# Third user of the score banks: row sums and Q and K products of attention move from the bank of turned probabilities into the ring of three score banks

## The chip, the cores and the metric

The kernel runs on one core of one Trainium2 chip. The metric is the device time of one execution in microseconds (us). PE is TensorE, ACT is ScalarE, DVE is VectorE, POOL is GpSimd and SP is SyncE.

## What is computed

The reference is two layers over X of 8 x 512 x 256 in fp32. Each layer computes `x = x + s * silu(f)`, with s from attention (layer 0) or a selective state-space scan (layer 1), and f from a mixture of 64 experts (layer 0) or a forest of 8 decision trees (layer 1). The change lies in the attention of layer 0, per batch b:

```
Q = (X @ Wq).reshape(n, s, NUM_GROUPS, HEADS_PER_GROUP, KEY_WIDTH)      # 16 heads of 64
K = (X @ Wk).reshape(n, s, NUM_GROUPS, KEY_WIDTH)                       # 4 groups of 64
V = (X @ Wv).reshape(n, s, NUM_GROUPS, VALUE_WIDTH)
raw = jnp.einsum('bsgwe,btge->bstgw', Q, K * scale)
attn = jax.nn.softmax(raw, axis=2)
A = jnp.einsum('bstgw,btge->bsgwe', attn, V).reshape(n, s, NUM_HEADS * VALUE_WIDTH)
return X + A @ Wpost
```

The mixture, the trees and the scan run beside it and are computed as before.

## The kernel before, in words

Every engine has its own instruction stream. One generator, `in_order`, walks through all parts of the work in one order and calls the method of the same name on each of the five engine classes, so every engine issues its share in that order. Semaphores join the engines; `Gate.wait_ge` (L66) leaves out a wait that an earlier one of the engine already covers. Attention and trees are the filler: `attention(b)` yields steps that are dealt out between the steps of routing, table and experts (batches 0 and 1) and of the scan (batches 2 to 7).

Attention of one batch works on 64 tiles: 16 heads of 512 queries, 128 queries at a time. Heads go in pairs, and a pair has 8 steps (`PAIR_STEPS`): step n is head j = n % 2 and query tile i = n % 8 // 2 of pair p = n // 8. PE issues most of its work at even n. Of tile m:

- score (L1702), in `score`: two products per even step, of tiles n and n + 1. They contract 64 rows each, head 0 on rows 0 to 63 and head 1 on rows 64 to 127. The profile has two matmul records for each.
- maximum (DVE L1184) and exponential (ACT L968), one step later (`LAG_EXP` = 1). The exponential writes Pr and frees the score's bank.
- turn (PE L1713, `turn_p`): four transposes of Pr into bank 3 (`PROBT`), two steps behind the score (`LAG_T` = 2). ACT copies the bank to PT (L988).
- values (PE L1725, `values`): products of PT with V for two tiles, into bank 4, four steps behind (`LAG_AV` = 4).

Scores go round a ring of three banks, 0 to 2 (`RING_S_ATT` = 3): tile m has bank m % 3, so its score waits for the exponential of tile m - 3.

Once or more in a pair another product is made, in `other`: at step 2 the spread of the reciprocal row sums of the pair before (L1736, four transposes of rowinv), which ACT copies to inv_bc (L978); at step 4 the Q product of the next pair (L1664, copied by ACT L951 to Qp); at step 6 of every second pair the K product of the next group (L1664, copied by L946 to Kp). Before, all of these go to bank 3 (`PROJ = PROBT`), between turns. Each therefore waits for the last PT copy, and the turn behind it waits for the copy of this product. At such steps the value products are cut in halves: chunks 0 and 1 between the other product and the turn, chunks 2 and 3 in the odd step before the next turn.

On ACT a step n issues: exponential n - 1, the copy of the other product if there is one, the copy of PT n - 2. Between the steps stand the decays of the scan (L1092), one exponential of 128 x 512 for each scan step.

Of the kernel before, what the change touches and what calls it, by code (L numbers as in the profile page):

```python
# [8 lines left out]
P = 128  # L9
TILES = SEQ // P  # L10
NT = NB * TILES
KC = DM // P
# [450 lines left out]
def build_program(nc, X, Wq, Wk, Wv, Wpost, gateT, gate_bias, w_gate, w_up, w_down, ln_gb, WinT, WxT, WdtT,  # L463
# [122 lines left out]
    PROBT, AV, SIDE = 3, 4, 5  # L586
    PROJ = PROBT
    K_LEAD, Q_LEAD = 0, 1
# [266 lines left out]
    def _(act):  # L855
# [7 lines left out]
        class Scalar(Parts):  # L863
# [79 lines left out]
            def copy_k(self, b, g, bk):  # L943
                w.wait_ge(att_kmm, GROUPS * b + g + 1)
                w.wait_ge(att_scored, ATT_STEPS // GROUPS * (GROUPS * b + g - 1))
                act.activation(Kp[:, g % 2, :], bank[bk][:, :], ACT.Copy, scale=HD ** -0.5).then_inc(att_k, 1)  # L946

            def copy_q(self, b, p, bk):
                w.wait_ge(att_qmm, PAIRS * b + p + 1)
                w.wait_ge(att_scored, PAIR_STEPS * (PAIRS * b + p - 1))  # L950
                act.copy(Qp[:, p % 2, :], bank[bk][:, :]).then_inc(att_q, 1)  # L951

            def att_lead(self, b, j):
                if j == 0:
                    self.copy_k(b, 0, K_LEAD)
                else:
                    self.copy_q(b, 0, Q_LEAD)

            def att_step(self, b, n):
                m = n - LAG_EXP  # L960
                if 0 <= m < ATT_STEPS:
                    p, i, j = att_place(m)
                    place = b * ATT_STEPS + m
                    w.wait_ge(att_max, place + 1)
                    w.wait_ge(att_turned, place - RING_P + 1 if m >= RING_P else b * ATT_STEPS)
                    if m < RING_P and b >= 2:
                        w.wait_ge(tree_proj, 2 * TREES * (b - 1))
                    act.activation(Pr[:, m % RING_P, :], bank[m % RING_S_ATT][:, :], ACT.Exp, bias=negmax[:, m % RING_STAT:m % RING_STAT + 1],  # L968
                                   accum_out=rowsum[:, p % 2, 2 * i + j:2 * i + j + 1]).then_inc(att_exp, 1)
                p, at = n // PAIR_STEPS, n % PAIR_STEPS  # L970
                if at == 1 and p >= 1:
                    w.wait_ge(att_rec, PAIRS * b + p)
                    w.wait_ge(att_invmm, PAIRS * b + p - 1)
                    act.copy(rowinv[:, :, :], wide(rowrec[:, :], [[1, PAIR_STEPS], [0, HD]])).then_inc(att_inv, 1)
                if at == 2 and p >= 1:
                    w.wait_ge(att_invmm, PAIRS * b + p)
                    w.wait_ge(att_at, PAIRS * b + p - 1)
                    act.copy(inv_bc[:, :], bank[PROJ][:, :]).then_inc(att_invbc, 1)  # L978
                if at == 4 and p + 1 < PAIRS:
                    self.copy_q(b, p + 1, PROJ)  # L980
                if at == 6 and p + 1 < PAIRS and p % 2:
                    self.copy_k(b, (p + 1) // 2, PROJ)
# [133 lines left out]
    def _(dve):  # L1116
# [38 lines left out]
        class Vector(Parts):  # L1155
# [24 lines left out]
            def att_step(self, b, n):  # L1180
                m = n - LAG_EXP
                if 0 <= m < ATT_STEPS:
                    w.wait_ge(att_scored, b * ATT_STEPS + m + 1)
                    dve.tensor_reduce(negmax[:, m % RING_STAT:m % RING_STAT + 1], bank[m % RING_S_ATT][:, :], AX.X, ALU.max, negate=True).then_inc(att_max, 1)  # L1184
                p, at = n // PAIR_STEPS - 1, n % PAIR_STEPS
# [429 lines left out]
    def _(pe):  # L1615
# [9 lines left out]
        class Tensor(Parts):  # L1625
# [36 lines left out]
            def product(self, weight, bk):  # L1662
                for c in range(KC):
                    ins = pe.matmul(bank[bk][:, :], weight[:, c, :], xaT[:, c, :], start=(c == 0), stop=(c == KC - 1))  # L1664
                return ins

            def product_k(self, b, g):
                w.wait_ge(att_q, PAIRS * b + 2 * g + 1)
                w.wait_ge(att_invbc, PAIRS * b + 2 * g - 1)
                w.wait_ge(att_pt, b * ATT_STEPS + PAIR_STEPS * (2 * g - 1) + 6 - LAG_T)  # L1670
                self.product(Wk_sb[:, :, g * P:(g + 1) * P], PROJ).then_inc(att_kmm, 1)

            def product_q(self, b, p):
                w.wait_ge(att_k, GROUPS * b + p // 2 + p % 2)
                w.wait_ge(att_invbc, PAIRS * b + p - 1)
                w.wait_ge(att_pt, b * ATT_STEPS + PAIR_STEPS * (p - 1) + 4 - LAG_T)
                self.product(Wq_sb[:, :, p * P:(p + 1) * P], PROJ).then_inc(att_qmm, 1)

            def att_lead(self, b, j):
# [4 lines left out]
                if j == 0:  # L1684
                    self.product(Wk_sb[:, :, 0:P], K_LEAD).then_inc(att_kmm, 1)
                else:
                    self.product(Wq_sb[:, :, 0:P], Q_LEAD).then_inc(att_qmm, 1)

            def score(self, b, n):
                for m in (n, n + 1):  # L1690
                    p, i, j = att_place(m)
                    if m >= RING_S_ATT:
                        w.wait_ge(att_exp, b * ATT_STEPS + m - RING_S_ATT + 1)
                    else:
# [6 lines left out]
                    own = slice(j * HD, (j + 1) * HD)  # L1701
                    pe.matmul(bank[m % RING_S_ATT][:, :], Qp[own, p % 2, i * P:(i + 1) * P], Kp[own, p // 2 % 2, :], start=True, stop=True).then_inc(att_scored, 1)  # L1702
# [12 lines left out]

            def values(self, b, m, chunks):
                p, i, _ = att_place(m)
# [4 lines left out]
                g = p // 2  # L1722
                for c in chunks:
# [3 lines left out]
                if c == TILES - 1:  # L1727
                    ins.then_inc(att_av, 1)

            def spread(self, b, p):  # L1730
                w.wait_ge(att_inv, PAIRS * b + p + 1)
                w.wait_ge(att_q, PAIRS * b + min(p + 2, PAIRS))
                w.wait_ge(att_k, GROUPS * b + min(p + 1, PAIRS - 1) // 2 + 1)
                w.wait_ge(att_pt, b * ATT_STEPS + PAIR_STEPS * (p + 1) + 2 - LAG_T)
                for i in range(TILES):
                    ins = pe.transpose(bank[PROJ][:, i * P:(i + 1) * P], whole(rowinv[:, 2 * i:2 * i + 2, :]), ident[:, :])  # L1736
                ins.then_inc(att_invmm, 1)

            def att_step(self, b, n):

                p, at = n // PAIR_STEPS, n % PAIR_STEPS
# [10 lines left out]
            def has_other(self, p, at):  # L1752
                return at == 2 and p >= 1 or at == 4 and p + 1 < PAIRS or at == 6 and p + 1 < PAIRS and p % 2 == 1

            def other(self, b, p, at):
                if at == 2 and p >= 1:
                    self.spread(b, p - 1)
                if at == 4 and p + 1 < PAIRS:
                    self.product_q(b, p + 1)
                if at == 6 and p + 1 < PAIRS and p % 2:  # L1760
                    self.product_k(b, (p + 1) // 2)
                return self.has_other(p, at)

# [245 lines left out]
```

## Time and profile before

| | us |
|---|---|
| median of 3 runs | 3165.19 |
| lowest, highest | 3160.37, 3168.80 |
| profiled execution, its own time | 3152.14 |
| its span | 3150.3 |
| busy PE, DVE, ACT, POOL | 2507.4, 2020.4, 1858.4, 1709.6 |
| granted TensorE clock, mean | 0.898 |

The profile is one execution. Busy time is the union of an engine's records. A wait is idle time of an engine, put down to what released it. The chain of waits is followed back from the last instruction.

### The profile page before, as it was taken

The page shows a single profiled execution, that of the slowest core. Times are in us where ns is not written, and L with a number is a line of the kernel's source. Part 1 is how long each engine was busy: PE and PEld are TensorE (multiplying, and loading weights), DVE is VectorE, ACT ScalarE, POOL GpSimd, SP SyncE. Part 2 cuts the span into 40 slices and gives each one's busy share as a digit, 9 for nine tenths or more (in the row PEclk, how much of TensorE's full clock was granted, in tenths as well). Part 3 has the DMA queues.
Part 4 walks back from the last instruction along what each step waited for, and adds up shares of the span by engine and source line. Part 5 has one row for each costly group of instructions (what it writes and reads, how often), then busy time and mean ns, then how long its engine had stood idle before and what let it go on. Part 6 is the DMA issues. An engine that isn't in the chain of part 4 may idle for free.

```text
span 3150.3 us, 37618 instructions
## 1 busy us (share of the span) xinstructions
PE 2507.4 (80%) x12740; PEld 1402.0 (45%) x12744; DVE 2020.4 (64%) x3019; ACT 1858.4 (59%) x3341; POOL 1709.6 (54%) x1400
## 2 busy tenths in 40 slices
PE   5786699996888887979897779888988987856662
PEld 3444377753444444445443434453445443532321
DVE  4878655533466667667775657476856665768686
ACT  3457534454667665776676456656775667645552
POOL 1000254347357775767775558575856585544454
PEclk9788899997889998999998889999988998988785
DMA  4000378844445565546643544345434543455575
GB/s 136 21 18 5 89 222 236 230 97 71 92 112 104 110 134 114 102 87 138 132 98 64 114 108 98 68 105 136 102 74 95 137 103 66 103 133 122 133 156 114
DMA packets 281008, 344.83 MB, mean 109 GB/s; under 512 B 81456, under 2 KB 210366, under 8 KB 280816
## 3 DMA queue, kind: packets, MB, share of 16 engines
q0 software_dynamic: 79872, 171.99, 29.5%
q1 hardware_dynamic: 178432, 148.86, 16.4%
q10 hardware_dynamic: 22512, 21.57, 2.0%
q8 instruction: 102, 1.67, 0.2%
q14 instruction: 90, 0.74, 0.1%
HBM read 198.10 MB, written 26.80 MB: 71 GB/s over the span
## 4 chain that ended last, share of the span: by engine, by line
PE 46%; ACT 17%; DVE 16%; issue 11%; SPq 4%; DMA 3%; POOL 3%; DVEq 0%; ACTq 0%; POOLq 0%; another core or an unknown queue 0%
PE bank L1713 8%; PE bank L1702 7%; PE bank L1664 5%; PE bank L1852 4%; PE bank L1771 3%; PE bank L1823 3%; PE bank L1725 3%; SPq L788 3%; ACT PT L988 3%; DVE bank L1497 3%; PE bank L1881 2%; ACT bank L1092 2%; ACT Pr L968 2%; DVE negmax L1184 2%; PE bank L1917 2%
## 5 line engine op out<-in xcount | busy, mean ns | idle before, releaser
L1593 POOL TENSOR_TENSOR arena<-arena 128x512 f32<-128x512 f32 x512 | 846.3, 1712 | 164.3 <-DMA arena<-bc_dram 100.3
L1497 DVE TENSOR_TENSOR_SCAN bank<-bank,arena 128x512 f32<-128x512 f32 x320 | 391.1, 1222 | 204.5 <-ACT bank L1092 180.8
L1599 POOL TENSOR_TENSOR arena<-arena 128x512 f32<-128x512 f32 x192 | 278.1, 1448 | 435.5 <-DVE arena L1497 400.0
L1577 POOL DMA_INDIRECT acc_sb<-ybuf,slot_idx x256 | 414.9, 1621 | 180.7 <-DMA ybuf<-arena 63.7
L1702 PE MATMUL bank<-Kp,Qp 64*128 64x512 f32 x1024 | 415.9, 692 | 87.8 <-ACT Pr L968 82.8
L1092 ACT ACTIVATE bank<-arena,A_sb 128x512 f32<-128x512 f32 x512 | 352.1, 693 | 216.0 <-DVE arena L1505 204.8
L1713 PE MATMUL bank<-ident,Pr 128*128 128x128 f32 x2048 | 360.6, 303 | 141.7 <-ACT PT L988 87.7
L968 ACT ACTIVATE Pr<-bank,negmax 128x512 f32<-128x512 f32 x512 | 353.2, 690 | 180.5 <-DVE negmax L1184 176.9
L1184 DVE TENSOR_REDUCE negmax<-bank 128x1 f32<-128x512 f32 x512 | 342.3, 678 | 156.8 <-PE bank L1702 156.3
L988 ACT COPY PT<-bank 128x512 f32<-128x512 f32 x512 | 299.7, 585 | 224.1 <-PE bank L1713 216.6
L1713 PEld LDWEIGHTS bank<-ident,Pr 128*128 128x128 f32 x2048 | 233.8, 150 | 325.1 <-issue 99.3
L1609 POOL DMA_DIRECT2D arena<-arena x256 | 264.1, 1032 | 156.2 <-DVE arena L1505 153.3
L1497 DVE TENSOR_TENSOR_SCAN arena<-bank,arena 128x512 f32<-128x512 f32 x192 | 233.4, 1216 | 164.0 <-ACT bank L1092 153.1
L1725 PE MATMUL bank<-PT,V_sb 128*64 128x128 f32 x4096 | 335.2, 298 | 4.1 <-DVE AT L1199 4.1
L1725 PEld LDWEIGHTS bank<-PT,V_sb 128*64 128x64 f32 x4096 | 233.8, 145 | 151.4 <-issue 143.4
L1568 POOL DMA_INDIRECT arena<-rows,arena x128 | 129.1, 1008 | 314.7 <-DVE arena L1374 210.9
L1505 DVE TENSOR_TENSOR arena<-bank,arena 128x512 f32<-128x512 f32 x320 | 218.5, 683 | 8.3 <-DMA arena<-bc_dram 3.7
L1702 PEld LDWEIGHTS bank<-Kp,Qp 64*128 64x128 f32 x1024 | 116.8, 198 | 216.8 <-ACT Pr L968 142.8
L1028 ACT ACTIVATE AT<-bank,ffn_b_sb 127x512 f32<-127x512 f32 (+1 forms) x128 | 87.0, 687 | 145.0 <-PE bank L1852 120.8
L1862 PE MATMUL bank<-PT,path_sb 127*127 127x512 bf16 (+1 forms) x128 | 52.7, 412 | 108.0 <-DVE Pr L1445 101.2
L1664 PE MATMUL bank<-xaT,Wq_sb 128*128 128x512 f32 x256 | 137.2, 661 | 0.0
L1823 PE MATMUL bank<-arena 128*128 128x256 f32 x512 | 124.4, 386 | 11.5 <-DVE arena L1403 11.5
(212 smaller groups left out, 4025.4 us busy)
## 6 DMA issues: line engine op xcount, KB each, us to landing
arena<-arena POOLq DMA_DIRECT2D x256, 512.0 KB, 5.4
arena<-bc_dram SPq DMA_DIRECT2D x256, 256.0 KB, 3.9
ybuf<-arena ACTq DMA_DIRECT2D x64, 256.0 KB, 3.9
arena<-in_w_gate SPq DMA_DIRECT2D x64, 128.0 KB, 3.0
arena<-in_w_up SPq DMA_DIRECT2D x64, 128.0 KB, 4.0
arena<-in_w_down SPq DMA_DIRECT2D x64, 128.0 KB, 4.7
arena<-in_X SPq DMA_DIRECT2D x8, 512.0 KB, 7.4
s_sb<-in_X SPq DMA_DIRECT2D x8, 512.0 KB, 9.3
```

Of the source, the lines that this page charges most:

```text
L968: act.activation(Pr[:, m % RING_P, :], bank[m % RING_S_ATT][:, :], ACT.Exp, bias=negmax[:, m % RING_STAT:m % RING_STAT + 1], accum_out=row ...
L988: act.copy(PT[:, m % RING_P, :, :].rearrange("p a b -> p (a b)"), bank[PROBT][:, :]).then_inc(att_pt, 1)
L1092: act.activation(bank[DECAY[g % 2]][:, :], dt_sb[:, size_slot(b, cb), :], ACT.Exp, scale=A_sb[:, cb, n:n + 1]).then_inc(ssm_decay, 1)
L1184: dve.tensor_reduce(negmax[:, m % RING_STAT:m % RING_STAT + 1], bank[m % RING_S_ATT][:, :], AX.X, ALU.max, negate=True).then_inc(att_max, 1)
L1497: dve.tensor_tensor_scan(v if c_by_pool(m) else decay, decay, v, 0.0, ALU.mult, ALU.add).then_inc(ssm_scan, 1)
L1577: pool.indirect_dma_start(acc_sb[:, i, :], None, ybuf, bass.IndirectOffsetOnAxis(ap=slot_idx[:, b * TILES + i, k:k + 1], axis=0), bounds_c ...
L1593: pool.tensor_tensor(st_sb[:, g % RING_S, :], u_sb[:, size_slot(b, cb), :], B_sb[:, load % RING_BC, :], ALU.mult).then_inc(ssm_input, 1)
L1599: pool.tensor_tensor(v, v, C_sb[:, load % RING_BC, :], ALU.mult).then_inc(ssm_c_pool, 1)
L1664: ins = pe.matmul(bank[bk][:, :], weight[:, c, :], xaT[:, c, :], start=(c == 0), stop=(c == KC - 1))
L1702: pe.matmul(bank[m % RING_S_ATT][:, :], Qp[own, p % 2, i * P:(i + 1) * P], Kp[own, p // 2 % 2, :], start=True, stop=True).then_inc(att_sco ...
L1713: ins = pe.transpose(bank[PROBT][:, c * P:(c + 1) * P], Pr[:, m % RING_P, c * P:(c + 1) * P], ident[:, :])
L1725: ins = pe.matmul(bank[AV][j * HD:(j + 1) * HD, i * P:(i + 1) * P], V_sb[:, c, g * HD:(g + 1) * HD], PT[:, (m + j) % RING_P, c, :], start= ...
```

## The change

The three banks 0 to 2 now serve scores, spreads and the later Q and K products in the order in which PE issues them (`score_users`); a user takes the next bank and waits until the user three places before it has been read. The first K and Q product of a batch stay in banks 0 and 1. Bank 3 holds turned probabilities alone. The value products are no longer cut in halves: all stand in the odd step, before its turn. The copies on ACT and the maxima on DVE read the bank that the list names.

```diff
+    def beside_scores(n):
+        p, at = n // PAIR_STEPS, n % PAIR_STEPS
+        if at == 2 and p >= 1:
+            return "spread", p - 1
+        if at == 4 and p + 1 < PAIRS:
+            return "q", p + 1
+        if at == 6 and p + 1 < PAIRS and p % 2:
+            return "k", (p + 1) // 2
+        return None
+
+    score_users = []
+    for n in range(0, ATT_STEPS + LAG_RAN, 2):
+        if n < ATT_STEPS:
+            score_users += [("score", n), ("score", n + 1)]
+        if beside_scores(n):
+            score_users.append(beside_scores(n))
+
+    def score_bank(kind, i):
+        return bank[score_users.index((kind, i)) % RING_S_ATT]
+
+    def score_bank_free(b, kind, i):
+        kind, i = score_users[score_users.index((kind, i)) - RING_S_ATT]
+        if kind == "score":
+            return att_exp, b * ATT_STEPS + i + 1
+        if kind == "spread":
+            return att_invbc, PAIRS * b + i + 1
+        if kind == "q":
+            return att_q, PAIRS * b + i + 1
+        return att_k, GROUPS * b + i + 1
...
             def product_q(self, b, p):
-                w.wait_ge(att_k, GROUPS * b + p // 2 + p % 2)
-                w.wait_ge(att_invbc, PAIRS * b + p - 1)
-                w.wait_ge(att_pt, b * ATT_STEPS + PAIR_STEPS * (p - 1) + 4 - LAG_T)
-                self.product(Wq_sb[:, :, p * P:(p + 1) * P], PROJ).then_inc(att_qmm, 1)
+                w.wait_ge(*score_bank_free(b, "q", p))
+                self.product(Wq_sb[:, :, p * P:(p + 1) * P], score_bank("q", p)).then_inc(att_qmm, 1)
...
                     if m >= RING_S_ATT:
-                        w.wait_ge(att_exp, b * ATT_STEPS + m - RING_S_ATT + 1)
+                        w.wait_ge(*score_bank_free(b, "score", m))
...
             def turn_p(self, b, m):
-                p, at = (m + LAG_T) // PAIR_STEPS, (m + LAG_T) % PAIR_STEPS
                 w.wait_ge(att_exp, b * ATT_STEPS + m + 1)
                 w.wait_ge(att_pt, b * ATT_STEPS + m)
                 w.wait_ge(att_v, 2 * (b + 1))
-                w.wait_ge(att_q, PAIRS * b + min(p + 1 + (at >= 4), PAIRS))
-                w.wait_ge(att_k, GROUPS * b + min(p + (at >= 6), PAIRS - 1) // 2 + 1)
-                w.wait_ge(att_invbc, PAIRS * b + (p - (at < 2) if p else 0))
...
                 if n % 2 == 0:
                     if n < ATT_STEPS:
                         self.score(b, n)
-                    if self.other(b, p, at) and 0 <= n - LAG_AV < ATT_STEPS:
-                        self.values(b, n - LAG_AV, (0, 1))
+                    self.other(b, n)
                 elif 0 <= n - 1 - LAG_AV < ATT_STEPS:
-                    self.values(b, n - 1 - LAG_AV, (2, 3) if self.has_other(p, at - 1) else (0, 1, 2, 3))
+                    self.values(b, n - 1 - LAG_AV)
```

The order on PE shows it in two places of batch 1. The first is a step with a Q product (step 44). Qp and Kp are the operands of scores, Pr that of turns, PT that of values, xaT that of the Q product. Before:

```order
L1702 MATMUL bank2<-Kp,Qp 128x512
L1702 MATMUL bank0<-Kp,Qp 128x512 [waits att_exp]
L1664 MATMUL bank3<-xaT,Wq_sb 128x512 [waits att_pt]
L1664 MATMUL bank3<-xaT,Wq_sb 128x512
L1725 MATMUL bank4<-PT,V_sb 64x128 [waits att_at]
L1725 MATMUL bank4<-PT,V_sb 64x128 x3
L1713 MATMUL bank3<-ident,Pr 128x128 [waits att_q]
L1713 MATMUL bank3<-ident,Pr 128x128 x3
L1725 MATMUL bank4<-PT,V_sb 64x128 x4
L1713 MATMUL bank3<-ident,Pr 128x128 [waits att_pt,att_exp]
L1713 MATMUL bank3<-ident,Pr 128x128 x3
```

Of the change, the same step:

```order
L1730 MATMUL bank2<-Kp,Qp 128x512 [waits att_exp]
L1730 MATMUL bank0<-Kp,Qp 128x512 [waits att_exp]
L1696 MATMUL bank1<-xaT,Wq_sb 128x512 [waits att_invbc]
L1696 MATMUL bank1<-xaT,Wq_sb 128x512
L1737 MATMUL bank3<-ident,Pr 128x128 [waits att_pt]
L1737 MATMUL bank3<-ident,Pr 128x128 x3
L1749 MATMUL bank4<-PT,V_sb 64x128 [waits att_at]
L1749 MATMUL bank4<-PT,V_sb 64x128 x7
L1737 MATMUL bank3<-ident,Pr 128x128 [waits att_pt]
L1737 MATMUL bank3<-ident,Pr 128x128 x3
```

The Q product has bank 1 in place of 3, the turn behind it no longer waits for att_q (its copy), and the eight value products stand together behind that turn. The second place is the next pair of scores (step 46) and what follows it, on PE as well, where a K product is the third user. Before:

```order
L1702 MATMUL bank1<-Kp,Qp 128x512
L1702 MATMUL bank2<-Kp,Qp 128x512 [waits att_exp]
L1664 MATMUL bank3<-xaT,Wk_sb 128x512 [waits att_pt]
L1664 MATMUL bank3<-xaT,Wk_sb 128x512
L1725 MATMUL bank4<-PT,V_sb 64x128 x4
L1713 MATMUL bank3<-ident,Pr 128x128 [waits att_k]
```

Of the change:

```order
L1730 MATMUL bank2<-Kp,Qp 128x512 [waits att_exp]
L1730 MATMUL bank0<-Kp,Qp 128x512 [waits att_exp]
L1696 MATMUL bank1<-xaT,Wk_sb 128x512 [waits att_q]
L1696 MATMUL bank1<-xaT,Wk_sb 128x512
L1737 MATMUL bank3<-ident,Pr 128x128 [waits att_pt]
```

Before, the score of tile 46 needs no wait of its own (exponential 43 has been waited for by turn 43), and that of tile 47 waits for exponential 44. In the change tile 46 takes the bank of tile 44 and waits for exponential 44, and tile 47 takes the bank of tile 45 and waits for exponential 45.

## Rows read from the trace of the kernel before

**Rows 1.** The page: shares of the chain that ended last, by engine.

```profile
PE 46%; ACT 17%; DVE 16%; issue 11%; SPq 4%; DMA 3%; POOL 3%; DVEq 0%; ACTq 0%; POOLq 0%; another core or an unknown queue 0%
```

**Rows 2.** Busy time by stretch, attention passes; length, busy us (xinstructions), granted clock, DMA share.

```profile
core 0: us, PE busy (x) PEld busy (x) DVE busy (x) ACT busy (x) POOL busy (x), PEclk, DMA share, GB/s
57.00:287.00 230.00, 175.35 (x1248) 99.32 (x1251) 181.94 (x439) 122.05 (x246) 3.63 (x6) 0.84 0.05 15
350.00:655.00 305.00, 265.09 (x1500) 201.40 (x1496) 146.35 (x305) 120.61 (x282) 129.05 (x128) 0.96 0.75 213
907.00:1086.00 179.00, 160.74 (x936) 82.05 (x934) 119.48 (x172) 125.29 (x267) 124.33 (x99) 0.95 0.50 100
...
2540.00:2750.00 210.00, 175.84 (x970) 91.78 (x967) 140.63 (x190) 137.52 (x281) 131.20 (x101) 0.89 0.41 85
sum 1696.00, PE 1450.16 PEld 816.12 DVE 1098.89 ACT 1049.18 POOL 937.13; mean PE 181.27 PEld 102.01 DVE 137.36 ACT 131.15 POOL 117.14
```

**Rows 3.** Chain of waits within 1886 to 2089 us, shares by line.

```profile
by line: PE bank L1702 16.1%; PE bank L1713 15.7%; PE bank L1664 10.9%; issue 8.7%; PE bank L1725 7.0%; ACT PT L988 4.8%; ACT bank L1092 4.0%; ACT Pr L968 3.4%; PE bank L1917 3.4%; DVE negmax L1184 2.6%; PE bank L1940 2.5%; ACT inv_bc L978 
```

**Rows 4.** Waits of PE over the span: total us, times, longest us.

```profile
PE bank L1713 <- ACT PT L988: 87.7, 135, 6.3
PE bank L1702 <- ACT Pr L968: 82.8, 47, 7.3
...
PE bank L1713 <- ACT inv_bc L978: 40.5, 21, 6.8
...
PE bank L1736 <- ACT PT L988: 12.0, 6, 4.4
```

**Rows 5.** Timeline, 1602 to 1606 us: start us, us, instruction, idle before it.

```profile
1603.40 0.69 ACT L968 ACTIVATE Pr<-bank,negmax 128x512 f32<-128x512 f32 x1 [1.12 <-DVE negmax L1184]
...
1604.08 0.57 ACT L988 COPY PT<-bank 128x512 f32<-128x512 f32 x1
...
1604.23 1.12 PE L1702 MATMUL bank<-Kp,Qp 64*128 64x512 f32 x2 [0.61 <-ACT Pr L968]
...
1604.59 0.69 ACT L968 ACTIVATE Pr<-bank,negmax 128x512 f32<-128x512 f32 x1
...
1605.28 0.65 PE L1713 MATMUL bank<-ident,Pr 128*128 128x128 f32 x4
...
1605.97 0.59 ACT L988 COPY PT<-bank 128x512 f32<-128x512 f32 x1 [0.60 <-PE bank L1713]
```

**Rows 6.** Chain of waits, 1614 to 1626 us: start us, us, what (a Q step).

```profile
1615.30 1.06 PE bank L1702 x4
1616.35 1.93 PE bank L1664 x4
...
1618.31 0.59 ACT Qp L951
...
1618.94 0.67 PE bank L1713 x4
...
1619.64 0.59 ACT PT L988
...
1620.37 0.63 PE bank L1713 x4
```

**Rows 7.** Groups of ACT within 1886 to 2089 us: count, busy us, mean ns, idle before.

```profile
L968 ACT ACTIVATE Pr<-bank,negmax 128x512 f32<-128x512 f32 x61 | 42.0, 688 | 8.5 <-DVE negmax L1184 8.3
...
L1092 ACT ACTIVATE bank<-arena,A_sb 128x512 f32<-128x512 f32 x39 | 27.2, 698 | 0.0
```

**Rows 8.** Timeline: value products of one step in one piece.

```profile
1605.87 1.09 PE L1725 MATMUL bank<-PT,V_sb 128*64 128x128 f32 x16
```

**Rows 9.** Busy time of two stretches of 50 us of one attention pass, columns as in rows 2.

```profile
2000.00:2050.00 50.00, 37.94 (x190) 18.65 (x191) 26.24 (x34) 34.58 (x65) 23.10 (x19) 0.84 0.25 53
...
1950.00:2000.00 50.00, 46.72 (x264) 23.02 (x264) 32.06 (x44) 33.97 (x73) 34.84 (x27) 1.00 0.39 82
```

More of the change, by code:

```diff
@@ L945, in copy_k @@
                 w.wait_ge(att_scored, ATT_STEPS // GROUPS * (GROUPS * b + g - 1))
-                act.activation(Kp[:, g % 2, :], bank[bk][:, :], ACT.Copy, scale=HD ** -0.5).then_inc(att_k, 1)
+                act.activation(Kp[:, g % 2, :], bk[:, :], ACT.Copy, scale=HD ** -0.5).then_inc(att_k, 1)
             def copy_q(self, b, p, bk):
@@ L950, in copy_q @@
                 w.wait_ge(att_scored, PAIR_STEPS * (PAIRS * b + p - 1))
-                act.copy(Qp[:, p % 2, :], bank[bk][:, :]).then_inc(att_q, 1)
+                act.copy(Qp[:, p % 2, :], bk[:, :]).then_inc(att_q, 1)
             def att_lead(self, b, j):
                 if j == 0:
-                    self.copy_k(b, 0, K_LEAD)
+                    self.copy_k(b, 0, bank[K_LEAD])
                 else:
-                    self.copy_q(b, 0, Q_LEAD)
+                    self.copy_q(b, 0, bank[Q_LEAD])
             def att_step(self, b, n):
@@ L967, in att_step @@
                         w.wait_ge(tree_proj, 2 * TREES * (b - 1))
-                    act.activation(Pr[:, m % RING_P, :], bank[m % RING_S_ATT][:, :], ACT.Exp, bias=negmax[:, m % RING_STAT:m % RING_STAT + 1],
+                    act.activation(Pr[:, m % RING_P, :], score_bank("score", m)[:, :], ACT.Exp, bias=negmax[:, m % RING_STAT:m % RING_STAT + 1],
                                    accum_out=rowsum[:, p % 2, 2 * i + j:2 * i + j + 1]).then_inc(att_exp, 1)
@@ L977, in att_step @@
                     w.wait_ge(att_at, PAIRS * b + p - 1)
-                    act.copy(inv_bc[:, :], bank[PROJ][:, :]).then_inc(att_invbc, 1)
+                    act.copy(inv_bc[:, :], score_bank("spread", p - 1)[:, :]).then_inc(att_invbc, 1)
                 if at == 4 and p + 1 < PAIRS:
-                    self.copy_q(b, p + 1, PROJ)
+                    self.copy_q(b, p + 1, score_bank("q", p + 1))
                 if at == 6 and p + 1 < PAIRS and p % 2:
-                    self.copy_k(b, (p + 1) // 2, PROJ)
+                    self.copy_k(b, (p + 1) // 2, score_bank("k", (p + 1) // 2))
                 m = n - LAG_T
@@ L1183, in att_step @@
                     w.wait_ge(att_scored, b * ATT_STEPS + m + 1)
-                    dve.tensor_reduce(negmax[:, m % RING_STAT:m % RING_STAT + 1], bank[m % RING_S_ATT][:, :], AX.X, ALU.max, negate=True).then_inc(att_max, 1)
+                    dve.tensor_reduce(negmax[:, m % RING_STAT:m % RING_STAT + 1], score_bank("score", m)[:, :], AX.X, ALU.max, negate=True).then_inc(att_max, 1)
                 p, at = n // PAIR_STEPS - 1, n % PAIR_STEPS
@@ L1684, in att_lead @@
                 if j == 0:
-                    self.product(Wk_sb[:, :, 0:P], K_LEAD).then_inc(att_kmm, 1)
+                    self.product(Wk_sb[:, :, 0:P], bank[K_LEAD]).then_inc(att_kmm, 1)
                 else:
-                    self.product(Wq_sb[:, :, 0:P], Q_LEAD).then_inc(att_qmm, 1)
+                    self.product(Wq_sb[:, :, 0:P], bank[Q_LEAD]).then_inc(att_qmm, 1)
             def score(self, b, n):
@@ L1701, in score @@
                     own = slice(j * HD, (j + 1) * HD)
[L1702 removed]
+                    pe.matmul(score_bank("score", m)[:, :], Qp[own, p % 2, i * P:(i + 1) * P], Kp[own, p // 2 % 2, :], start=True, stop=True).then_inc(att_scored, 1)
             def turn_p(self, b, m):
[L1705 removed]
                 w.wait_ge(att_exp, b * ATT_STEPS + m + 1)
@@ L1714, in turn_p, with values @@
                 ins.then_inc(att_turned, 1)
[L1716 removed]
+            def values(self, b, m):
                 p, i, _ = att_place(m)
@@ L1722, in values @@
                 g = p // 2
-                for c in chunks:
+                for c in range(TILES):
                     for j in range(2):
@@ L1744, in att_step, with other @@
                         self.score(b, n)
-                    if self.other(b, p, at) and 0 <= n - LAG_AV < ATT_STEPS:
-                        self.values(b, n - LAG_AV, (0, 1))
+                    self.other(b, n)
                 elif 0 <= n - 1 - LAG_AV < ATT_STEPS:
-                    self.values(b, n - 1 - LAG_AV, (2, 3) if self.has_other(p, at - 1) else (0, 1, 2, 3))
+                    self.values(b, n - 1 - LAG_AV)
                 if 0 <= n - LAG_T < ATT_STEPS:
                     self.turn_p(b, n - LAG_T)
[L1752 to L1762, printed above, removed]
+            def other(self, b, n):
+                kind, i = beside_scores(n) or (None, 0)
+                if kind == "spread":
+                    self.spread(b, i)
+                if kind == "q":
+                    self.product_q(b, i)
+                if kind == "k":
+                    self.product_k(b, i)
             def att_post(self, b, i):
```

19 lines of the change are left out of this document (6 added, 13 removed).

## The prediction, written before the change was timed

> **What bounds the kernel now.** I read the page first, then the busy time of each stretch that holds an attention pass, then the chain of waits inside such a stretch, and last single instructions. The chain that ended last lies on PE for 46% of the span, on ACT for 17% and on DVE for 16% [rows 1]. The eight attention passes can be told apart by when the score products (L1702) run. The first (57 to 287 us) lies beside normalising, routing and the table. The second lies mostly beside the experts (350 to 655 us). The other six, 907 to 1086 us up to 2540 to 2750 us, lie beside the scan of an earlier batch and fill 1696 - 230 - 305 = 1161 us together [rows 2]. In the first and the last of the six PE is busy 90% and 84% of the time, ACT 70% and 65%, POOL 69% and 62% [rows 2]. In one of them (1886 to 2089 us) the chain goes by turns through scores, turning of probabilities, products and ACT's copies of PT; DVE and POOL hardly appear [rows 3]. So in these six passes PE and ACT hand work to each other, and what delays PE there delays nearly everything.
>
> PE still waits. Over the span it sat idle 82.8 us before scores for an exponential, 87.7 us before turns for the last PT copy, 40.5 us before turns for inv_bc, and 12.0 us before spreads for PT [rows 4]. The last two come from the sharing of bank 3 that the change ends. The first comes from the ring of three score banks, which the change makes tighter.
>
> **Part 1, what is added: a later exponential to wait for.** After a step with a third user of the ring (spread at 2, Q at 4, K at 6 of a pair's eight steps), the next two scores take the banks of the two scores just before that user. Score n then waits for exponential n-2, and score n+1 for exponential n-1; before it was n-3 and n-2. On ACT exponential n-1 stands behind the copy of PT n-3, and that copy waits for turn n-3, the last thing that PE does before score n. So a fixed run lies between the end of a turn and score n+1. The rows give each link [rows 5]: a turn ends at 1605.28 + 0.65 = 1605.93 us and its copy starts at 1605.97 (0.04 us); a copy starts at 1604.08 and the exponential behind it at 1604.59 (0.51 us); an exponential takes 0.69 us; one ends at 1603.40 + 0.69 = 1604.09 us and its score starts at 1604.23 (0.14 us). Sum 0.04 + 0.51 + 0.69 + 0.14 = 1.38 us. DVE's maximum of that score is not in it, since the score was made two steps earlier.
>
> Nothing hides this. The two scores of a step are heads j = 0 and 1, on different row halves of the array. With no wait between them both together take 1.06 us in the chain [rows 6], and one alone takes 1.12 us [rows 5]. So score n under the wait of score n+1 saves nothing: a pair that went in one piece now ends 1.38 + 1.12 - 1.06 = 1.44 us later.
>
> ACT also carries the decays of the scan. In the stretch from 1886 us there are 39 of them beside 61 exponentials, 0.70 us each (27.2 / 39) [rows 7]. They fall between ACT's attention steps, the very gap that is now waited for, so a pair gets 39 / 61 x 0.70 = 0.45 us more on average. That makes 1.44 + 0.45 = 1.89 us.
>
> How many pairs: in a batch the pair of scores follows a spread 7 times (the eighth lies behind the last score), a Q product 7 times and a K product 3 times, 17 in all, 136 in 8 batches. 136 x 1.89 = 257 us.
>
> Off this comes what those pairs lose already. PE idled 47 times and 82.8 us before scores [rows 4], and each such pair also ran one after the other, 1.12 + 1.12 - 1.06 = 1.18 us more than together: 82.8 + 47 x 1.18 = 138 us over all pairs. Of the 31 pairs of a batch that wait for the ring at all, 17 are the affected ones, so 17 / 31 of it, 76 us, is contained in the new wait. Added: 257 - 76 = 181 us. Its bounds: if the decays always hide and the old waits fall all on affected pairs, 136 x 1.44 - 138 = 58 us; if none of the old waits is contained, 257 us. I take 181, worked from the averages.
>
> **Part 2, what is taken away: the round trip through bank 3.** At 1616.35 us a Q product takes 1.93 us and ends at 1618.28; copy, turn, PT copy and second turn end at 1620.37 + 0.63 = 1621.00 us, 2.72 us later [rows 6]. Both halves of the value products lie under the two copies. In the new order, third user, turn (0.67), all value products (1.09 for the sixteen records [rows 8]), turn (0.63), nothing waits for the copy of the third user and the PT copy is covered by the value products: 0.67 + 1.09 + 0.63 = 2.39 us, and less by the overlap of about 0.06 that modelled ends show at each join (0.65 shown, 0.60 in the chain). I take 2.72 - 2.39 = 0.33, plus 0.06 for the overlap, 0.39 us. It happens at 18 third users of a batch (8 spreads, 7 Q, 3 K), 144 times: 56 us. Bounds: nothing, if ACT is late anyway; or with the long waits for inv_bc and for PT before spreads wholly gone as well, 56 + 40.5 + 12.0 = 109 us. Those long waits (up to several us) are ACT being behind with work of the scan, and with the copy no longer asked for, PE is stopped two scores later by the exponential in the same queue. So I add nothing for them.
>
> The rest costs nothing: the same matmuls, copies and maxima are issued, on the same queues, and only the place of four value products moves (behind the turn). SP and POOL get no other order. The copies of Q, K and inv_bc read another bank for the same length. The spread now waits for an exponential n-1 too, with two scores (1.06 us) as cover, and loses at most 0.3 us, seven times a batch: 17 us at the most, inside the bounds. Q waits for inv_bc and K for Q, each copied two steps before.
>
> **Part 3, the sum.** 181 - 56 = +125 us, if all of it reaches the end. It doesn't in the first two passes, a quarter of it (31 us): from 57 to 287 us DVE is busier than PE (181.94 against 175.35 us), and from 350 to 655 us the DMA queues are 0.75 busy with weights [rows 2]; I let a third through (10 us). Of the other 94 us nearly all passes; together about 100 us. The profiled execution took 3152.1 us (span 3150.3 and 1.8 around it), so it would be 3252; the median of the runs is 3165.2, 13 above that execution, which gives **3265 us**.
>
> **The clock.** From 1950 to 2000 us PE is busy 46.72 us of 50 and the granted clock is 1.00; from 2000 to 2050 us, busy 37.94, it is 0.84, so part of that stretch ran at 1.2 instead of 2.4 GHz [rows 9]. New stalls of 1 to 2 us each, with matmuls on both sides, are short beside those that such stretches hold, so my sum has no term for it. The Trainium skill, page TensorE: Matmul & The Clock Gate, section "A second HAM failure mode: psum-queue depth-cycling", says that cycling through PSUM banks each iteration lets TensorE idle for moments often enough that the clock swings between its levels. By that rule, which speaks against this change, the clock term would not be zero; it is the third rival.
>
> **The rivals.**
> - *Most of the stall is absorbed.* Where ACT or DVE is late anyway, PE only moves its wait from the turn to the score, and the time comes near the lower bound of part 1, 58 - 56, plus some. For it: ACT is busy 65% to 70% of the stretches itself. Against it: the chain there is PE and its turns. Half of the 100 us would give about 3215 us. Chance 0.17.
> - *Faster: the exponential is never late.* If between turn n-3 and score n+1 enough other PE work lies (products of the scan's input), the 1.38 us run is covered, and only part 2 stays. It decides from 1.4 us of such work at each place, against a turn followed at once by scores as at 1620.37 and 1621.00 us. Price -56 us: 3152 - 56 + 13 = about 3109 us. Chance 0.07.
> - *The clock falls too.* If the six passes fell from their 0.89 to 0.95 [rows 2] by 0.07, as towards the 0.84 of the stretch above, PE would lose 0.07 x 1161 = 81 us more: about 3345 us. Chance 0.15. (The page's rule would bring this about.)
> - *No change that can be told*: both terms near their low ends. Chance 0.05.
>
> My forecast has the rest, 0.56. A measurement of this kernel tells about 0.3% (9 us) from no change. Faster 0.07, same 0.06, slower 0.87. The range takes in the absorbed case and the clock case: 3195 to 3350 us.
>
> **What would show it.** In the changed profile the wait "L1730 for Pr (L968 before)" should grow from 82.8 us and 47 times to some 130 us and over 120 times, the two scores behind a third user should run 1.1 us each, apart, and waits for inv_bc, Qp and Kp at turns should be gone. PT waits before turns should fall from 135 times. PE's busy time should rise by some 100 us with unchanged work, since lone scores replace pairs. The attention stretches should each be 12 to 18 us longer, the stretches of the trees as long as before. I am wrong if scores still run in pairs there, if the six stretches are no longer, or if the clock carries the difference.

## The result, and the profile after

The changed kernel takes 3407.25 us (median of 4 runs, 3401.22 to 3418.22), against 3166.99 us for the kernel before in the same comparison. The ratio is 1.0765, with a 95% interval of 1.073 to 1.080. I had forecast 3265 us, with a range up to 3350. The direction was right and the size was not: the loss is 242 us (0.0765 x 3167) where I had 100.

The page of the changed kernel: span, busy time of the engines, granted clock in 40 slices, and the chain by engine.

```profile
span 3416.4 us, 37434 instructions
...
PE 2656.7 (78%) x12740; PEld 1486.7 (44%) x12744; DVE 2025.8 (59%) x3019; ACT 1854.0 (54%) x3341; POOL 1710.1 (50%) x1400
...
PEclk9787799998998999989887888888988998888786
...
PE 50%; ACT 18%; DVE 13%; issue 9%; SPq 3%; DMA 2%; POOL 2%; another core or an unknown queue 1%; ACTq 0%; DVEq 0%; POOLq 0%
```

DVE, ACT and POOL are busy as long as before. PE is busy 149 us longer (2507.4 before) with the same 12740 records, and its share of the chain rose from 46% [rows 1] to 50%.

The waits of PE in the changed kernel (us in total, times, longest us), against [rows 4]:

```profile
PE bank L1730 <- ACT Pr L1000: 217.0, 151, 7.3
...
PE bank L1757 <- ACT Pr L1000: 65.4, 41, 7.5
...
PE bank L1737 <- ACT PT L1020: 44.9, 25, 6.4
```

The wait of scores (L1730, before L1702) for an exponential grew from 82.8 us and 47 times to 217.0 us and 151 times. The waits of turns (L1737) for inv_bc, Qp and Kp are gone, and that for PT fell from 135 times to 25. There is one that I had put at 17 us at the most: spreads (L1757) wait 65.4 us for an exponential.

Busy time by stretch, for the first two attention passes, the first and the last beside the scan, and the longest; columns as in [rows 2]:

```profile
61.00:313.00 252.00, 187.15 (x1220) 105.54 (x1224) 183.35 (x439) 120.13 (x242) 3.64 (x6) 0.81 0.04 13
364.00:811.00 447.00, 375.71 (x2125) 261.34 (x2114) 187.66 (x374) 184.52 (x416) 184.80 (x165) 0.91 0.59 157
971.00:1178.00 207.00, 175.33 (x934) 92.83 (x933) 118.35 (x172) 123.70 (x266) 125.05 (x100) 0.89 0.43 87
...
1661.00:1907.00 246.00, 199.18 (x940) 100.29 (x940) 131.16 (x174) 138.40 (x283) 142.56 (x111) 0.81 0.35 71
...
2774.00:3016.00 242.00, 191.01 (x969) 102.01 (x970) 140.56 (x189) 136.61 (x280) 131.59 (x101) 0.86 0.35 73
```

The same passes in the kernel before, from its first score to its last:

```profile
61.00:287.00 226.00, 171.35 (x1224) 96.34 (x1228) 181.94 (x439) 120.39 (x243) 3.63 (x6) 0.84 0.05 15
340.00:742.00 402.00, 347.29 (x2121) 246.71 (x2114) 187.07 (x374) 185.41 (x418) 183.95 (x165) 0.95 0.66 175
906.00:1085.00 179.00, 160.73 (x934) 82.36 (x936) 119.48 (x172) 124.79 (x266) 124.18 (x100) 0.95 0.50 101
...
1535.00:1734.00 199.00, 169.65 (x942) 85.31 (x942) 125.86 (x174) 138.86 (x284) 141.28 (x111) 0.91 0.43 86
...
2539.00:2749.00 210.00, 175.84 (x970) 91.98 (x970) 139.86 (x190) 137.52 (x282) 131.90 (x101) 0.89 0.41 85
```

All eight passes together went from 1789 to 2057 us. These 268 us are the whole difference of the two spans (266 us; the two profiled executions lie a little further apart than the medians), so all of the loss lies in attention. The first two passes lost 26 and 45 us, the six others 23 to 47 us each. And the granted clock fell in every one: in the rows above from 0.84 to 0.81, 0.95 to 0.91, 0.95 to 0.89, 0.91 to 0.81 and 0.89 to 0.86. Over the span it fell from 0.898 to 0.870. The stretches that the trace records at 1.2 GHz, the lower of the two levels, add up to 648 us before and 887 us now.

One late pair in full, from the timeline of the changed kernel (start us, us, what):

```profile
1405.55 0.66 PE L1737 MATMUL bank<-ident,Pr 128*128 128x128 f32 x4
...
1406.14 1.12 PE L1730 MATMUL bank<-Kp,Qp 64*128 64x512 f32 x2
1406.25 0.59 ACT L1020 COPY PT<-bank 128x512 f32<-128x512 f32 x1 [0.29 <-PE bank L1737]
...
1406.73 0.70 ACT L1124 ACTIVATE bank<-arena,A_sb 128x512 f32<-128x512 f32 x1
...
1407.35 0.68 ACT L1000 ACTIVATE Pr<-bank,negmax 128x512 f32<-128x512 f32 x1
...
1408.17 1.12 PE L1730 MATMUL bank<-Kp,Qp 64*128 64x512 f32 x2 [0.91 <-ACT Pr L1000]
1408.23 1.22 DVE L1529 TENSOR_TENSOR_SCAN arena<-bank,arena 128x512 f32<-128x512 f32 x1
1409.23 1.98 PE L1696 MATMUL bank<-xaT,Wq_sb 128*128 128x512 f32 x4
```

The turn ends at 1406.21 us, ACT copies it, a decay of the scan (L1124) comes next, then the exponential, and the second score starts at 1408.17: 1.96 us behind the turn, where part 1 of the prediction has 1.38 plus a decay of 0.70. The first score used 1.1 us of that and gained nothing by it.

### The profile page after: what moved, and what is told of

Read it like the earlier page. It is cut to its first block, busy times and chain, and to the rows that moved or that the text cites. A ratio compares the mean times of both kernels' runs of the same rounds, so it can differ in the third digit from the quotient of the medians.

```text
span 3416.4 us, 37434 instructions
## 1 busy us (share of the span) xinstructions
PE 2656.7 (78%) x12740; PEld 1486.7 (44%) x12744; DVE 2025.8 (59%) x3019; ACT 1854.0 (54%) x3341; POOL 1710.1 (50%) x1400
## 4 chain that ended last, share of the span: by engine, by line
PE 50%; ACT 18%; DVE 13%; issue 9%; SPq 3%; DMA 2%; POOL 2%; another core or an unknown queue 1%; ACTq 0%; DVEq 0%; POOLq 0%
PE bank L1730 8%; PE bank L1737 6%; PE bank L1696 6%; PE bank L1749 5%; PE bank L1868 5%; ACT Pr L1000 4%; ACT bank L1124 3%; PE bank L1897 3%; PE bank L1787 3%; PE bank L1839 3%; ACT PT L1020 2%; DVE bank L1529 2%; SPq L820 2%; PE bank L1933 2%; DVE negmax L1216 1%
## 5 line engine op out<-in xcount | busy, mean ns | idle before, releaser
L1730 PE MATMUL bank<-Kp,Qp 64*128 64x512 f32 x1024 | 531.8, 713 | 225.0 <-ACT Pr L1000 217.0
L1124 ACT ACTIVATE bank<-arena,A_sb 128x512 f32<-128x512 f32 x512 | 352.9, 694 | 224.0 <-DVE arena L1537 210.3
L1737 PE MATMUL bank<-ident,Pr 128*128 128x128 f32 x2048 | 372.8, 311 | 45.0 <-ACT PT L1020 44.9
L1737 PEld LDWEIGHTS bank<-ident,Pr 128*128 128x128 f32 x2048 | 258.2, 157 | 257.7 <-issue 191.8
L1730 PEld LDWEIGHTS bank<-Kp,Qp 64*128 64x128 f32 x1024 | 142.9, 204 | 436.1 <-ACT Pr L1000 374.0
L1749 PE MATMUL bank<-PT,V_sb 128*64 128x128 f32 x4096 | 323.4, 307 | 0.0
L1749 PEld LDWEIGHTS bank<-PT,V_sb 128*64 128x64 f32 x4096 | 254.6, 154 | 78.2 <-issue 77.2
L1696 PE MATMUL bank<-xaT,Wq_sb 128*128 128x512 f32 x256 | 162.3, 767 | 12.3 <-ACT Pr L1000 12.3
L983 ACT COPY Qp<-bank 128x512 f32<-128x512 f32 x64 | 37.5, 586 | 216.2 <-PE bank L1696 216.2
```

What stands on the lines that cost most here:

```text
L1124: act.activation(bank[DECAY[g % 2]][:, :], dt_sb[:, size_slot(b, cb), :], ACT.Exp, scale=A_sb[:, cb, n:n + 1]).then_inc(ssm_decay, 1)
L1696: ins = pe.matmul(bk[:, :], weight[:, c, :], xaT[:, c, :], start=(c == 0), stop=(c == KC - 1))
L1730: pe.matmul(score_bank("score", m)[:, :], Qp[own, p % 2, i * P:(i + 1) * P], Kp[own, p // 2 % 2, :], start=True, stop=True).then_inc(att_s ...
```

## The experiments

The theory after the first look: the later exponential makes the loss in two ways, directly (stall and lone scores) and through the clock. The rivals: the loss comes from the bank changes or the order of the value products, or the clock costs nothing by itself. Ratios are to the kernel before, run on the same chip; a difference between two runs is taken from their ratios. The clock is that of the profiled execution alone. It differs from one execution to the next (0.870 to 0.873 for the change, 0.874 to 0.882 with the joint wait, 0.891 to 0.901 with two repeats) and from chip to chip: for the kernel before it is 0.898 in the profile, and its median is 0.901, 0.902, 0.899 and 0.899 on the four chips of the other runs. A step of 0.004 in this column, some 25 us at the lower clock, therefore tells nothing.

| run | what | ratio (95% interval) | clock |
|---|---|---|---|
| the change | | 1.0765 (1.073 to 1.080) | 0.870 |
| w1_late_wait | before, later wait only | 1.1008 (1.0969 to 1.1047) | 0.875 |
| w2_spread_back | change, spreads in bank 3 | 1.0523 (1.0487 to 1.0558) | 0.883 |
| w3_products_back | change, Q and K in bank 3 | 1.0365 (1.0327 to 1.0404) | 0.892 |
| f1_filled | change, stall filled once | 1.0618 (1.0584 to 1.0652) | 0.891 |
| f2_filled_twice | change, stall filled twice | 1.0763 (1.0728 to 1.0798) | 0.901 |
| g1_filled_spread | f1, and before spreads | 1.0685 (1.0653 to 1.0717) | 0.890 |
| j1_joint_wait | change, pair waits together | 1.0781 (1.0732 to 1.083) | 0.882 |
| r1_turn_first | change, turn before values | 1.0587 (1.0564 to 1.061) | 0.886 |
| d1_values_whole | before, values in one piece | 1.0099 (1.0065 to 1.0132) | 0.899 |
| c1_products_last | Q and K in the ring, issued late | 0.9965 (0.9947 to 0.9984) | 0.895 |
| c2_q_last | only Q so | 1.0019 (1.0006 to 1.0032) | 0.892 |
| c3_k_last | only K so | 0.9955 (0.9941 to 0.9969) | 0.905 |

**The wait alone.** The list `score_users` is put into the kernel before and used for the scores' wait only; banks, order and the other waits stay.

```diff
                     if m >= RING_S_ATT:
-                        w.wait_ge(att_exp, b * ATT_STEPS + m - RING_S_ATT + 1)
+                        w.wait_ge(att_exp, b * ATT_STEPS + max(exps_before(m), m - RING_S_ATT + 1))
```

> The kernel before with one thing of the change: the scores behind a third user wait for the later exponential (n-2 and n-1), though their banks and all else stay. Theory (the later exponential makes the loss, directly and through the clock): the whole loss of the change or more, since the gain at bank 3 is missing but the spread's own wait too: 1.06 to 1.10 of the kernel before, half-clock time of TensorE up from 648 us to 850 us or more. Rival (the third user in the ring or the order of the value products costs, not this wait): under 1.03.

Measured: 1.1008, just above the range that I expected, with 860 us at the lower clock. Its waits of PE:

```profile
PE bank L1717 <- ACT Pr L983: 228.6, 150, 7.3
...
PE bank L1728 <- ACT PT L1003: 53.9, 66, 6.4
PE bank L1728 <- ACT inv_bc L993: 38.0, 21, 6.8
```

The scores wait 228.6 us in 150 places, as in the changed kernel, and the loss is larger than that of the change. So the wait is enough to make the loss, and the rival falls. The difference to the change, 1.1008 - 1.0765 = 0.024 or 77 us, is what leaving bank 3 and the new order gave, less what the spread's new wait took.

**Which user costs what.** In the first run the spread goes back to bank 3, in the second the Q and K products do, each with its old waits and halved value products.

```diff
     def score_bank(kind, i):
+        if kind == "spread":
+            return bank[PROBT]
         return bank[score_users.index((kind, i)) % RING_S_ATT]
...
-        if beside_scores(n):
+        if beside_scores(n) and beside_scores(n)[0] != "spread":
             score_users.append(beside_scores(n))
```

> The changed kernel with the spreads back in bank 3 (with their waits and halved value products there); Q and K products stay in the ring. Theory: the 7 late pairs behind a spread and the spread's own wait for an exponential go, the 10 behind Q and K stay: 1.03 to 1.055 of the kernel before. Rival (the spread's wait, 65 us, is a small part and the rest is in Q and K): 1.06 or more.

> The changed kernel with Q and K products back in bank 3; only the spreads go through the ring. Theory: 7 late pairs of 17 and the spread's own wait stay: 1.02 to 1.045 of the kernel before, and together with the run that has the spreads back about the whole loss of the change. Rival (the loss needs both users in the ring, since a pair behind one user is followed by the next): the two losses together are under half of it.

Measured: 1.0523 with Q and K in the ring, 1.0365 with the spreads in it, both as the theory had them. The two losses add up to 0.089, a little more than the 0.0765 of both together. Each user brings its own late pairs; it does not need the other. By count, clock and gains included, the ring costs 0.0523 x 3146 / 80 = 2.1 us for a Q or K product, and 0.0365 x 3146 / 56 = 2.0 us for a spread.

**The clock.** While the second score waits, the first is computed again with the same operands into the same bank, and its semaphore is raised by the last copy.

```diff
-                    pe.matmul(score_bank("score", m)[:, :], Qp[own, p % 2, i * P:(i + 1) * P], Kp[own, p // 2 % 2, :], start=True, stop=True).then_inc(att_scored, 1)
+                    again = 1 if m == n and n >= 4 and beside_scores(n - 2) else 0
+                    for _ in range(again + 1):
+                        ins = pe.matmul(score_bank("score", m)[:, :], Qp[own, p % 2, i * P:(i + 1) * P], Kp[own, p // 2 % 2, :], start=True, stop=True)
+                    ins.then_inc(att_scored, 1)
```

> The changed kernel with a useless repeat of the first score of each late pair (same operands, same bank, 136 more products of some 1 us) while the second score waits. Theory that the lower clock carries about half of the loss: TensorE is kept busy in the stall, half-clock time falls from 887 us by 100 us or more, and the time falls by 30 to 90 us although more is computed. Rival (the clock follows and costs nothing, the stall is all): the same time or up to 60 us more.

> The changed kernel with two useless repeats of the first score of each late pair. One repeat (about 1 us) just fits into the stall; the second stands in the way. Theory: at full clock each late pair is about 0.6 us longer than with one repeat, so 40 to 90 us slower than that run, with half-clock time no more than 60 us lower than its 734 us. Rival (more filling still buys clock): as fast or faster than with one repeat.

Measured: with one repeat 1.0618, 0.0147 or 47 us faster than the changed kernel, although 136 products more are computed; 734 us at the lower clock in place of 887. With two repeats 1.0763, 46 us slower than with one, 665 us at the lower clock in its profiled execution, which was 17 us faster than its median. That is 69 us less than with one repeat, where I had expected no more than 60. I cut the six passes beside the scan into stretches from one odd turn to the next. In the 66 stretches in which neither the kernel before, the change, the wait alone nor the single repeat was at the lower clock, they sum to 400.9 us in the changed kernel and to 402.3 us with the repeat: at full clock the repeat costs nothing and gives nothing. Over all 174 stretches it is 1275 against 1225 us, with 328 against 201 us at the lower clock. So 127 us less at the lower clock gave back 50 us, about 0.4 us for each; by the whole span 47 / 153 = 0.3. The executions on record give a like price without any change of kernel: among the 123 of them, each held against those of the same kernel on the same chip, 1 us more at the lower clock goes with 0.29 us more time. What the single repeat gained it gained where the clock was low, so the clock is a term of its own, and the rival falls.

**The limits of this reading.** In one run another repeat, of the second score, stands before each spread. In another, both scores of a late pair wait for the exponential of the second, as here:

```diff
+                if n >= 4 and beside_scores(n - 2):
+                    w.wait_ge(*score_bank_free(b, "score", n + 1))
                 for m in (n, n + 1):
```

> The changed kernel with the repeat in the late pairs and one more repeat, of the second score, before each spread, where TensorE waits 65 us in all for an exponential. Theory of the clock as a term: 10 to 30 us faster than with the repeats in the late pairs alone, half-clock time under its 734 us. Rival (the spread's stalls are long ones, behind a late ACT, where the repeat costs its own time or nothing): 0 to 15 us slower.

> The changed kernel, but both scores of a late pair wait together for the exponential that the second needs. The pair then runs at once on both row halves and ends when it ended before (1.38 + 1.06 us behind the turn in place of 1.38 + 1.12), but TensorE is idle 1 us longer in each of 136 places. Theory that the clock is a term of its own: slower than the changed kernel by 20 to 80 us, half-clock time well above 887 us. Rival (only the end of the pair counts): the same as the changed kernel within 10 us.

Both went against the theory. The repeat before the spread made the kernel 0.0067 or 21 us slower than one repeat alone, with 747 against 734 us at the lower clock, too close to tell apart. It also holds back the semaphore of the second score, and with it that score's maximum; whether this is the cost was not tried. The joint wait is the same as the change (1.0781 and 1.0765, overlapping), as its rival had it, and its time at the lower clock is not above 887 us but 802. In its waits PE is idle far longer:

```profile
PE bank L1732 <- ACT Pr L1000: 366.1, 159, 9.9
```

That is 149 us more idle time before scores than the 217.0 us of the changed kernel, PE's busy time falls to 2480.5 us, and still the clock is not lower (0.882 against 0.870; the kernel before ran at 0.902 on this run's chip, so some of the step is the chip's). So idle time alone does not say how the clock falls. The two kernels differ in that the scores run at once on both row halves here and one at a time there. That the lone scores lower the clock is my guess and was not tried alone. Why the better clock gained no time here stays open too, and the price of the clock is the weaker for it.

**Cover for the exponential.** In the odd step behind a third user the turn goes before the value products.

> The changed kernel with one move on TensorE: in the odd step behind a third user the turn stands before the value products, so that these (1.09 us) lie between the turn and the next scores and cover most of the 1.38 us of copy and exponential; the turn then waits openly for the PT copy before it (0.69 us less nothing). Theory: about 0.4 to 1.0 us less at each of 136 late pairs, pairs run together again more often, and the clock recovers: 60 to 140 us faster than the changed kernel, 1.03 to 1.055 of the kernel before. Rival (the bank itself or the spread's wait carries the loss): within 30 us of the changed kernel.

Measured: 1.0587, 56 us faster than the changed kernel, just outside what the theory gave (60 to 140 us, up to 1.055) and clear of the rival. Two waits have changed places:

```profile
PE bank L1730 <- ACT Pr L1000: 144.8, 86, 5.9
PE bank L1737 <- ACT PT L1020: 121.5, 134, 6.3
```

Scores wait 86 times in place of 151, and turns 134 times in place of 25: the value products can cover one run or the other.

**The value products alone.** The kernel before with all value products behind the turn.

> The kernel before with the value products in one piece behind the turn, as in the change, and the third users still in bank 3. The turn behind a third user now waits openly for its copy (0.6 us), in 144 places, and the next turn no longer waits for PT. Theory: 0 to 0.2 us net at each place and some clock: 1.00 to 1.02 of the kernel before. It says how much of the change's gain at bank 3 came from the bank and how much from the order of the value products.

Measured: 1.0099, 31 us slower. In bank 3 the halves are worth having, so the gain in the change can't come from the order alone: it needs the bank.

**A version from the reasons.** The products that cause the late pair are issued where they cover it: behind the odd turn, in front of the next scores, with ACT's copy one even step later. The spread stays in bank 3. K moves to the start of its pair.

```diff
-        if at == 6 and p + 1 < PAIRS and p % 2:
+        if at == 0 and p + 1 < PAIRS and p % 2:
             return "k", (p + 1) // 2
...
+                if n % 2 and not self.halved(n - 1):
+                    self.other(b, n - 1)
```

> A version made from the reasons: spreads stay in bank 3 as before; Q and K products go through the score ring, but are issued at the end of the odd step, behind its turn, so that their 1.9 us cover the 1.4 us of copy and exponential before the next scores; ACT copies them one even step later, behind the exponential; K moves to the start of its pair. Theory: the 10 products of a batch cause no late pair and lose their round trip through bank 3 (0.4 us each): 20 to 60 us faster than the kernel before (0.98 to 0.993), with half-clock time at or under 648 us. Rival (ACT is late anyway at these places, or its later copies push out PT): 0.997 to 1.02.

> Only the Q products go through the score ring, issued at the end of the odd step behind its turn; spreads and K products stay in bank 3 as in the kernel before. The version with K there too came out at 0.9965. Theory: seven of ten products of a batch keep their gain, and K at its old place spares the waits that its move to the start of a pair brought (scores waited 110 us for exponentials there, 83 in the kernel before): 0.988 to 0.996. Rival (the gain is eaten at the Q products themselves): 0.996 to 1.003.

> Only the K products go through the score ring, issued at the end of the first odd step of their pair and copied one even step later; Q products and spreads stay in bank 3 as in the kernel before. With Q and K so placed the kernel came out at 0.9965, with Q alone at 1.0019. Theory (K carries the gain, 24 products only, about 0.5 us each and some clock): 0.992 to 0.998. Rival (the two moves help only together, since they pull products and spread apart): 0.999 to 1.003.

Measured: 0.9965 with both, between my two cases and near the rival, with 659 us at the lower clock where I had expected 648 at the most; 1.0019 with Q alone, where the rival was right; 0.9955 with K alone, as the theory had it, 14 us faster than the kernel before. K alone has the lowest ratio of this study, though its interval overlaps that of both together. Its clock was 0.903 in the median, against 0.899 for the kernel before on the same chip, which is too small a step to build on. Its waits:

```profile
PE bank L1733 <- ACT Pr L1002: 93.4, 52, 10.4
PE bank L1743 <- ACT PT L1022: 85.3, 107, 6.3
...
PE bank L1743 <- ACT inv_bc L1012: 30.8, 16, 6.0
```

They are near [rows 4] (52 waits of scores where the change has 151): a product issued in front of the exponential that is asked for makes the ring nearly free. Whether K gains by the ring or by its new place in the pair was not told apart.

## Why the prediction was wrong

The mechanism was right: the scores wait for an exponential in 151 places where it was 47, those behind a third user run alone, the waits at bank 3 are gone, and all of it lies in the attention passes. What failed is the clock, which I put at nothing, the third that I let through in the first two passes, the price of the spread's wait and the size of part 2. Step by step:

- *Part 1, the late pair.* Right in its links and, at full clock, in its size. In the 84 stretches of the six passes where neither kernel was at the lower clock, those behind a Q product with no product in the next step grew from 4.3 to 5.7 us, and those behind a spread, with a Q product in the next step (which gains at bank 3), from 6.7 to 7.2. Weighted by how often each kind comes in the six passes, all kinds give about 80 us at full clock, where parts 1 and 2 gave 94, with nothing for the spread. The same reckoning for the wait alone, which has late pairs and nothing else, gives 134 us, against 181 x 3 / 4 = 136 from part 1.
- *"The spread now waits for an exponential n-1 too ... and loses at most 0.3 us."* This step failed. The wait is the same 1.38 us run with the same decays, and two scores cover 1.06 us of it: 1.38 + 0.45 - 1.06 = 0.77 us, 56 times, 43 us. I had written the cover and left the decays out. Measured: 65.4 us, 41 times.
- *Part 2.* The gain of leaving bank 3 was undersized. The run with the wait alone is 77 us slower than the change, and that is already less the spread's wait. With the 43 to 65 us of that wait the gain is some 120 to 140 us; I had 56, inside bounds of 0 to 109. I had added nothing for the long waits, and those for inv_bc (40.5 us) are gone. The two errors have opposite signs and together make my 125 us 21 too high, so neither is why the loss was larger than forecast.
- *Part 3, "I let a third through".* This failed. The first two passes lost 26 and 45 us, more than the 31 of my whole sum, where I had 10. A busy share of DVE or of the DMA queues above PE's did not cover a stall of PE: of the 45 us, 41 arise beside the experts, where the queues are 0.75 busy, and PE spent 43 us more at the lower clock there. I take it that the other engines get their work in the same order behind PE; that was not tried.
- *"My sum has no term for it": the clock.* This is the largest miss. 239 us more of the time ran at 1.2 GHz; at the 0.3 to 0.4 us of the run with the repeats that is some 70 to 95 us. It was my third rival, priced at 81 us and given 0.15. I weighed one stall against the long ones of [rows 9] and not 136 of them with a lone score on either side. The rule of the Trainium skill, TensorE: Matmul & The Clock Gate, "A second HAM failure mode: psum-queue depth-cycling", that short idle moments between groups let the clock swing, agrees with this trace in its direction: the clock went from 0.898 to 0.870, and came back to 0.891 when the moments were filled. The joint wait, with more idle time and a clock of 0.882, shows that the length of the moments is not all of it.

The corrected sum: 181 us for the late pairs, less the 77 us that bank 3 and the spread's wait together measured, and 70 to 95 us for the clock, in all 174 to 199 us, against 242 measured. So 43 to 68 us stay without a cause that is shown. In the six passes they lie where the clock was low: the stretches lost 191 us, 80 by their growth at full clock, and the other 111 come with 177 us more at the lower clock, 0.6 us for each. A score record takes 589 ns at the shortest and 1220 at the longest, twice that, so by this estimate 1 us at the lower clock loses at most 0.5 us of work. Then the stalls themselves must be longer in those stretches; by how much, and whether the clock costs more there than the repeats gave back, stays open.

## What to carry to other kernels

When a buffer gets another user, count for each user behind it which earlier result it now waits for, and where that result stands in its engine's queue; the distance from there to the wait must be covered by work in between, and a product put into that gap costs next to nothing (1.0019 for 56 Q products) where the same product before the gap costs 2 us. Apply the same run to every wait that the change adds, also to the one that looks covered. And price a row of short stalls on TensorE with the clock: here an estimated third of the loss, or more, was not the stalls but the work around them at 1.2 GHz.

## What the runs showed of the hardware that I had not expected

- Useless work made the kernel faster: 136 repeats of a score product took 47 us off, with the granted clock at 0.891 in place of 0.870. A second set took the profiled execution to 0.901 and gave the 47 us back.
- More idle time did not bring a lower clock: with the pairs waiting together PE idled 366.1 us in place of 217.0 before scores, and the clock was 0.882 in place of 0.870 (0.874 to 0.882 against 0.870 to 0.873 over the executions, on a chip where the kernel before ran 0.004 higher).
- Two scores on different row halves with no wait between them take about as long as one (1.06 us in the chain of [rows 6], 1.12 us alone in [rows 5]). A wait for only one of them makes PE busy longer and gains no time: its busy time rose by 149 us with the same number of matmuls, part of it at the lower clock, and with the pairs waiting together it fell to 2480.5 us at the same ratio.
